# Transposing and weighing attention probabilities later in the slot, in a fused encoder-decoder layer

## The reference, cut to what matters

```
x = x + attention(q, k, v of layernorm(x), mask_self) @ w_ao + b_ao
x = x + attention(q of layernorm(x), k and v of ctx, mask_cross) @ w_co + b_co
x = x + gelu(layernorm(x) @ w1 + b1) @ w2 + b2

attention: scores = q.k / sqrt(32); scores = scores * mask - 10000 * (1 - mask)
           softmax(scores over keys) . v, head by head
```

## Time and profile before

| what | value |
|---|---|
| median of three runs | 1813.92 us (1811.06 to 1816.85) |
| profiled execution, its own time | 1812.26 us |
| its span, first to last instruction | 1810.4 us |
| TensorE (PE) busy | 1702.9 us, 94% |
| VectorE (DVE) busy | 1030.0 us, 57% |
| ScalarE (ACT) busy | 1039.1 us, 57% |
| GpSimd (POOL) busy | 658.4 us, 36% |
| mean granted TensorE clock | 0.987 of 2.4 GHz |

### The profile page before, as it was taken

The page is one execution under the profiler, slowest core; times in us unless marked ns, Lnnn a source line. Parts: engine busy times, 40 slices in busy tenths (PEclk is TensorE's granted clock), DMA queues, the critical chain, the costliest instruction groups (busy, mean ns, idle before and its releaser), DMA issues. The chain is left out here.

```text
span 1810.4 us, 40174 instructions
## 1 busy us (share of the span) xinstructions
PE 1702.9 (94%) x13342; PEld 1035.0 (57%) x13342; DVE 1030.0 (57%) x3584; ACT 1039.1 (57%) x3138; POOL 658.4 (36%) x812
## 2 busy tenths in 40 slices
PE   3899999999988999999999986999999999999999
PEld 2567676767656766766766653444444444444444
DVE  6877777777765677777777763633232333324221
ACT  3577787778876777777778864532323232323332
POOL 0456565565644554554655642202020202010110
PEclk9999999999999999999999996999999999999999
DMA  4432222222221232332223221320101010102010
GB/s 137 120 111 75 87 96 87 86 83 86 92 76 51 75 109 87 109 108 89 97 91 98 86 68 52 124 70 12 58 12 58 12 58 12 64 6 70 0 47 24
DMA packets 83236, 130.31 MB, mean 72 GB/s; under 512 B 14144, under 2 KB 22336, under 8 KB 83136
## 3 DMA queue, kind: packets, MB, share of 16 engines
q1 hardware_dynamic: 83136, 129.04, 22.3%
HBM read 103.83 MB, written 25.17 MB: 71 GB/s over the span
## 5 line engine op out<-in xcount | busy, mean ns | idle before, releaser
L1239 POOL TENSOR_TENSOR a_p_s<-a_p_s,a_rcp 128x512 f32<-128x512 f32 x256 | 266.0, 1039 | 479.3 <-DVE a_rcp L886 479.2
L755 ACT ACTIVATE a_p_s<-a_t_s,a_mx 128x128 f32<-128x128 f32 x1024 | 398.6, 396 | 9.7 <-DVE a_mx L877 9.7
L1420 PE MATMUL m_ps_y<-w,m_g_r 128*128 128x512 f16 x1536 | 353.2, 379 | 0.0
L1406 PE MATMUL m_ps_h<-mlp_xT,w 128*128 128x512 f16 x1536 | 349.8, 379 | 1.7 <-PEq L407 1.7
L1505 DVE SCALAR_TENSOR_TENSOR m_g_r<-m_g_t,up_by,m_g_r 128x512 f16<-128x512 f32 x128 | 103.2, 806 | 406.6 <-ACT m_g_r L1478 406.3
L1406 PEld LDWEIGHTS m_ps_h<-mlp_xT,w 128*128 128x128 f16 x1536 | 150.2, 98 | 181.6 <-issue 2.2
L1420 PEld LDWEIGHTS m_ps_y<-w,m_g_r 128*128 128x128 f16 x1536 | 150.3, 98 | 176.5
L877 DVE CUSTOM_DVE_ANT_0 a_t_s<-a_ps_s,a_m_add 128x128 f32<-128x128 f32 x1024 | 230.6, 281 | 6.4 <-DVE a_ps_s L867 6.1
L1461 ACT ACTIVATE m_g_t<-m_ps_h,bias_cols,back 128x512 f32<-128x512 f32 x128 | 99.3, 776 | 222.6 <-PE m_ps_h L1406 222.6
L867 DVE TENSOR_TENSOR a_ps_s<-a_ps_s,a_m_mul 128x512 f32<-128x512 f32 x256 | 176.4, 689 | 58.8 <-PE a_ps_s L539 58.5
L746 ACT COPY a_pT<-a_ps_t 128x512 f32<-128x512 f32 x256 | 148.8, 581 | 103.1 <-PE a_ps_t L548 103.0
(11 more groups left out here) (118 smaller groups left out, 2267.7 us busy)
## 6 DMA issues: line engine op xcount, KB each, us to landing
w_stage<-in_w SPq DMA_DIRECT2D x64, 256.0 KB, 3.1
a_x_t<-in_x SPq DMA_DIRECT2D x32, 256.0 KB, 2.8
a_res_t<-in_x SPq DMA_DIRECT2D x32, 256.0 KB, 2.9
x_after_self<-a_y_t SPq DMA_DIRECT2D x32, 256.0 KB, 2.0
w_stage<-in_ctx SPq DMA_DIRECT2D x32, 256.0 KB, 2.9
a_x_t<-x_after_self SPq DMA_DIRECT2D x32, 256.0 KB, 2.8
a_enc_t<-in_ctx SPq DMA_DIRECT2D x32, 256.0 KB, 3.4
a_res_t<-x_after_self SPq DMA_DIRECT2D x32, 256.0 KB, 2.8
```

Of the source, the lines that this page charges most:

```text
L755: last = nc.scalar.activation(p_s[:, n % 2, j], t_s[:, n % 2, j], ACT.Exp, scale=-1.0, bias=mx[:, n % 2, j:j + 1], accum_out=sums[:, n % 2 ...
L1239: nc.gpsimd.tensor_tensor(p_s[:, n % 2], p_s[:, n % 2], rcp[:, n % 2].unsqueeze(2).to_broadcast([P, HQ, P]), ALU.mult).then_inc(s["normal" ...
L1406: last = nc.tensor.matmul(ps_h[j % 2][:], w1[hw][:, j // KC, kc, (j % KC) * P:(j % KC + 1) * P], xT[:, hx, kc], start=(k == 0), stop=(k == ...
L1420: last = nc.tensor.matmul(ps_y[b][:], g_r[:, j % 2, hg, b * P:(b + 1) * P], w2[hw][:, j // KC, j % KC], start=(j == 0 and x == 0), stop=(j ...
```

## The change

Seven things are moved:

- `p_s`, `sums` and `rcp` get four places (`KC`) in place of two, and `exponent`, `invert_sums` and `normalise` wait for the slot four before in place of two before.
- `transpose_probs` handles slot n - 3 and comes in the middle of the slot, after the first half and the first flips.
- `weigh_values` comes at the end of slots 6 and 2, after the second half or the queries.
- ScalarE: `exponent` first, then the copy of keys, then `copy_probs`; `high_context` after the copies of values and queries.
- VectorE: `invert_sums` of slot 1 before `output_row`; `low_context` after the flip and the look; the statistics of the first row of a group move from slot 0 to slot 7 of the group before; the norms of group 1 move from before slot 0 of group 0 into it.
- `flips`: in the last group of self-attention the flips of x move ahead of the second half; at the end of attention the two last pairs move ahead too.
- SyncE: the two loads of x, both in slot 7 before, come in slots 5 and 7.

```diff
-            p_s = buf("p_s", [P, 2, HQ, P])
+            p_s = buf("p_s", [P, KC, HQ, P])
...
-                    return [("x", *at_end[g, n])] if last and (g, n) in at_end else []
+                    return [("x", *inside[g, n])] if not last and (g, n) in inside else []
...
-                    return [("x", g + 1, n - 2), ("enc", g + 1, n - 2)] if last and n in (2, 3) else []
+                    return [("enc" if last else "x", g + 1, n - 2)] if n in (2, 3) else []
...
-                        if n == 7 and norms_ahead(g + 1):
+                        if n in (5, 7) and g != -1 and norms_ahead(g + 1):
...
-                            load_x(g + 3, 0)
-                            load_x(g + 3, 1)
+                            load_x(g + 3, b)
...
-                        if n == 2 and prev or n == 6 and cur:
-                            for k in range(KC):
-                                weigh_values(*lag(g, n, 6 - k))
                         for what, k, b in flips(g, n, nxt, False):
                             (flip_x if what == "x" else flip_enc)(k, b)
+                        if cur if n >= 3 else prev:
+                            transpose_probs(*lag(g, n, 3))
...
-                        if cur if n >= 2 else prev:
-                            transpose_probs(*lag(g, n, 2))
+                        if n == 2 and prev or n == 6 and cur:
+                            for k in range(KC):
+                                weigh_values(*lag(g, n, 6 - k))
...
-                        if n >= 2 or known(g, 1):
-                            act.wait_ge(s["pt_done"], at(slot_no(*lag(g, n, 2))))
-                            act.wait_ge(s["inverted"], at(slot_no(*lag(g, n, 2))))
+                        if n >= KC or known(g, 1):
+                            act.wait_ge(s["pt_done"], at(slot_no(*lag(g, n, KC))))
+                            act.wait_ge(s["inverted"], at(slot_no(*lag(g, n, KC))))
...
-                        if cur if n >= 3 else prev:
-                            copy_probs(*lag(g, n, 3))
                         if cur if n >= 1 else prev:
                             exponent(*lag(g, n, 1))
                         if n >= 4 and nxt:
                             copy_cols(g + 1, n - 4, WK, k_t, "k_done", "k_copied")
-                        if n == 2 and prev:
-                            high_context(g - 1, 1)
-                        if n == 6 and cur:
-                            high_context(g, 0)
+                        if cur if n >= 3 else prev:
+                            copy_probs(*lag(g, n, 3))
...
+                        if n == 2 and prev:
+                            high_context(g - 1, 1)
+                        if n == 6 and cur:
+                            high_context(g, 0)
...
-                        if ahead and g != -1:
+                        if (g, n) == (0, 0):
+                            statistics(1, 0)
+                            for k in (0, 1, 4, 5, 6, 7):
+                                norm_part(1, k)
+                        elif (g, n) == (0, 2):
+                            statistics(2, 0)
+                            norm_part(2, 0)
+                        elif (g, n) == (0, 3):
+                            norm_part(2, 1)
+                        elif ahead and g != -1 and (g, n) != (0, 1):
                             norm_part(g + 2, n)
-                        elif ahead and n == 7:
-                            for k in range(NS):
-                                norm_part(1, k)
+                        if n == 7 and g != -1 and norms_ahead(g + 1):
+                            statistics(g + 3, 0)
```

More of the change, by code:

```diff
@@ L293, in flips @@
                 if not nxt:
-                    at_end = {(gN - 1, 4): (gN, 0), (gN - 1, 5): (gN, 1), (gN, 0): (gN + 1, 0), (gN, 1): (gN + 1, 1)}
-                    return [("x", *at_end[g, n])] if last and (g, n) in at_end else []
+                    inside = {(gN - 1, 4): (gN, 0), (gN - 1, 5): (gN, 1), (gN, 0): (gN + 1, 0), (gN, 1): (gN + 1, 1)}
+                    return [("x", *inside[g, n])] if not last and (g, n) in inside else []
                 if not crosses(g + 1):
@@ L498, in slot @@
                             load_res(g, n // 6)
-                        if n == 7 and norms_ahead(g + 1):
+                        if n in (5, 7) and g != -1 and norms_ahead(g + 1):
+                            b = n // 7
                             if isinstance(g, int) and g in (NG - 3, gN - 3):
-                                for b in range(GB):
-                                    sp.wait_ge(stored[b], 16 * (NG - 4 if g == NG - 3 else NG + 3))
-                            load_x(g + 3, 0)
-                            load_x(g + 3, 1)
+                                sp.wait_ge(stored[0], 16 * (NG - 4 if g == NG - 3 else NG + 3))
+                                sp.wait_ge(stored[1], 16 * (NG - 4 if g == NG - 3 else NG + 3))
+                            load_x(g + 3, b)
                         if (g, n) == (0, 0):
@@ L510, in slot @@
                         pass_piece(g, n)
+                        if (g, n) == (0, 0):
+                            load_x(2, 0)
+                            load_x(2, 1)
                     for b in range(GB):
@@ L547, in transpose_probs @@
                         for j in range(HQ):
-                            last = nc.tensor.transpose(ps_t[:, j], p_s[:, n % 2, j], ident[:])
+                            last = nc.tensor.transpose(ps_t[:, j], p_s[:, n % KC, j], ident[:])
                         last.then_inc(s["pt_done"], 1)
@@ L955, in slot @@
                             scale_scores(g, n)
+                        if n == 1 and prev:
+                            if cur:
+                                dve.wait_ge(s["scaled"], at(slot_no(g, n)))
+                            invert_sums(*lag(g, n, 2))
                         if n in (1, 4) and prev:
@@ L961, in slot @@
                             dve.sem_inc(s["mask_begun"], 1)
-                        if n % KC and (cur if n >= 2 else prev):
+                        if n % KC and (cur if n >= 2 else prev and n != 1):
                             if cur:
@@ L967, in slot @@
                             mask_scores(g, n)
+                        for what, k, b in flips(g, n, nxt, False):
+                            (flip_x if what == "x" else flip_enc)(k, b)
+                        if cur or prev or n < 4:
+                            split_weights(g, n)
                         if n == 2 and prev:
@@ L971, in slot @@
                             low_context(g, 0)
-                        for what, k, b in flips(g, n, nxt, False):
-                            (flip_x if what == "x" else flip_enc)(k, b)
-                        if cur or prev or n < 4:
-                            split_weights(g, n)
                         for what, k, b in flips(g, n, nxt, True):
@@ L979, in slot @@
                             split_weights(g, n)
-                        if ahead and g != -1:
+                        if (g, n) == (0, 0):
+                            statistics(1, 0)
[7 more added lines that the diff above has]
+                        elif ahead and g != -1 and (g, n) != (0, 1):
                             norm_part(g + 2, n)
-                        elif ahead and n == 7:
-                            for k in range(NS):
-                                norm_part(1, k)
+                        if n == 7 and g != -1 and norms_ahead(g + 1):
+                            statistics(g + 3, 0)
                     def norm_part(g, n):
                         if n == 0:
-                            statistics(g, 0)
                             statistics(g, 1)
@@ L1256, in slot @@
                             prepare_mask(g + 1, 0)
-                        if n == (2 if g != -1 else 7) and norms_ahead(g):
+                        if (g, n) == (0, 0):
+                            root(1, 0)
+                            root(1, 1)
+                        if n == (2 if g != 0 else 4) and g != -1 and norms_ahead(g):
                             root(g + 2, 0)
```

18 lines of the change are left out of this document (9 added, 9 removed).

## The result

The changed kernel takes 1853.62 us (median of 4 runs, 1852.74 to 1859.39), the kernel before 1813.78 beside it (4 runs, 1811.06 to 1816.85): a ratio of 1.0226, 95% interval 1.0199 to 1.0252. It is slower, as forecast, but by 40 us and not by 14; 1853.6 lies above the range of 1813 to 1841. All of it is in the attention part: from the first product of the feed-forward part to the end both kernels take 684 us.

A forecast was written before the change was run, and what follows sets the result against it. TensorE's queue was taken to set the pace. Regular groups 23.5, plus 1.8 + 3.4 + 0.4 - 0.8 - 1.1 - 2.9 - 2.5 - 7.5, sum to +14.3 us: forecast 1828, range 1813 to 1841.

The forecast's parts named there:

- (a): Slot 3: outputs of b = 1 wait 1.60 us after weighing for the context; net +1.20 self, +1.11 cross a group.
- the clock falls in each group: Rival: recurring waits slow TensorE's clock, 1.5 us lost in each of 29 groups, 44 more, 1872 us; chance 0.05.
- (b): Scores wait 1.00 us for the last queries' copy, with no transposition left to cover it: +0.44 us in every group.
- (c): First queries wait for `y_done`, and a transposition now stands between: -0.30 us in self, -0.15 in cross groups.
- (d): TensorE's wait for GpSimd ends with half a slot more and four places: -0.95 us cross, -0.20 self a group.
- (e): Cross groups: second encoder flip comes long after the first, so its wait goes: -0.43 us, and -0.20 for smaller edges.
- (f): Slot 1 of cross: values wait for slot 0's flip, whose copy follows `copy_probs`: a new gap of 0.85 us.
- (g): Seven groups with a weight split on ScalarE: +0.25 us each, 1.8; also groups 14, 30 and 31: +3.4.
- (h): Opening: first scores' masking now comes ahead of group 1's norms: -1.1 us, bounds 0 and -3.7.
- (i): Change of stage: waits in groups 15 and 16 go, bias products run at full clock: -2.9 and -2.5 us.
- (j): End of attention: last scores to last outputs take 23.8 us instead of 31.3: -7.5, bounds -4 and -11.
- the ends give back more: Rival: full clock lasts through opening, change of stage and end; another 12 us come back, 1816 us; chance 0.12.

## Why the prediction fell short, step by step

**The step that failed is (a)**, twice over. Its bounds were "1.5 (both engines at once on it) to 1.8 (each finishing another copy, 0.1 each)". The wait is 2.13. I asked what ScalarE would be busy with when the weighing ends, and not what it would be waiting for: the instruction in front of the context was itself released by the weighing, so a whole copy (0.5) stands behind the event and not a rest of one. With the copy behind the context the wait was 1.67 and both periods came out as forecast to 0.05 (32.50 for 32.45, 34.02 for 34.03). In groups 1 to 13 and 17 to 29 this is 6.0 + 6.4 = 12 us.

Its second half is a rival that the prediction held at 0.05: **the clock falls in each group**. It did, in 9 of groups 1 to 13 and in none of 17 to 29, at 1.6 a time: 14.5 to 15 us. The price of 1.5 was right; 29 groups and 1872 were too many. A clock below 1.00 in the steady part was also one of the prediction's own signs of being wrong. It set the rival aside because "single gaps of 1.49 left the clock at full in places", and that was half of what its rows say. The gap of 1.49 before 539.97 left it at full (1.00 from 541 to 544), but behind the same gap before 546.74 the clock fell, in the kernel before:

```profile
547.00:549.00 2.00, 2.00 (x32) 1.74 (x34) 0.72 (x2) 1.45 (x4) 0.00 (x0) 0.54 0.04 8
```

Thirty-two products of scores took 2.09 there in place of 1.17.

The Trainium skill, "TensorE: Matmul & The Clock Gate", section "HAM oscillation — how this bites in real kernels", describes a loop in which a wait for DMA of about 3 to 5 us slows the clock anew in every round. The waits here are shorter than those, so the 1872 that the prediction puts down to that rule does not follow from the page. The trace shows the same kind of loss at 1.99 to 2.06 idle in 9 self groups (0.78 and 0.65 in the windows behind one wait); in groups 17 to 29, and in groups 1 to 13 with 1.60 or less idle, it shows none (1.00).

**(b)** The 1.00 in front of the scores came as forecast. That it would be the queries' copy alone was half the truth: VectorE's maxima became just as late, through the context of slot 6, to which no step had given a price. **(c)** Right: the queries of slot 4 follow the transposition at once in self, with 0.2 in cross. **(d)** Right: GpSimd's share of TensorE's waits is 3.9 in place of 31.2. What it missed is that a part of this gain was to be had by inverting the sums first, without moving anything on TensorE: alone, that took these waits from 31.2 to 23.7 and the kernel to 1799. **(e)** No second wait of an encoder flip is left in the steady part, as forecast. **(f)** 0.91 for 0.85; undone by itself, 0.92 a period.

**(g)** The 3.4 for groups 14, 30 and 31 is a slip: with their neighbours' prices it would be 1.14 + 0.67 + 0.67 = 2.5. Groups 30 and 31 took 3.1 more than before; with the context first, groups 1 to 13 took 13.8 more than before and 17 to 29 took 8.9 more, against 14.8 (with a little more for the split groups) and 8.7. **(h)** Nothing came back: +0.5 to the first scores of group 1, where -1.1 and +0.4 were forecast. TensorE did get to the bias products sooner (51.74, at full clock), but stood 3.90 later, at the x flip of 59.69. **(i)** The bias products do run at full clock, but the stretch from group 14 to 17 gave 1.8, with 4.3 forecast; each of the three groups has the longer context wait in it. **(j)** 22.5 where 23.8 was worked out, and the last products at full clock give 2.0 more: -10.8 for -7.5. The nearness of 22.5 and 23.8 is partly luck: 23.8 was worked out at half clock, and in this stretch the clock was down for a part only (1.00 from 1140 to 1145, 0.71 from 1145 to 1150, 0.98 from 1150 to 1165). The rival **"the ends give back more"** was thus right about the full clock in the bias products and the last products, but the opening gave nothing back for it.

The distance of 27 us is thus: values' copy +12.4, clock +14.7, change of stage +2.5, opening +1.2, end -3.3: +27.5, for 41.0 - 14.3 = 26.7 to explain. The 0.8 between them is left to the small terms.

The rival **"the wait of (a) is covered"** was worth more than its 0.10 as a thing to build: with the wait covered the change is at 1810.7 (the rival had 1798), and at 1797 with the gap of (f) closed too. **"ScalarE becomes the bound"** did not happen: with the same work on ScalarE, the order alone took the kernel to 1824 and in the end to 1779.

## What to carry to other kernels

Where a step is moved to the end of a slot, look at each engine's queue at the instruction in front of the one that reads the result, and ask which event frees that one: if it is the same event, its whole length lies in the wait, and swapping the two can take it out (here 30 us for two lines). The same holds for what stands behind: an engine that waits in order holds back work which feeds a third engine, and it shows as a late release somewhere else (here the maxima, 5 us on). When two releases come at about the same time, undoing one shows little (0.18 of 0.44 a group here); mend both before the cause is called refuted. And take a change apart: this one was 40 us slower as a whole, and held an order of two instructions worth 14 and flips at the ends worth 9.

## What the runs showed of the hardware

Of TensorE's clock: behind an idle time of 1.99 to 2.06 in each of the self groups 1 to 13 of the change it fell in 9 and stayed at full in 4. With 1.60 or 1.47 (a flip before it) and a period of 32.5 it fell in none of them. But the kernel with the weighing alone moved has the same idle time in each self group, with more besides, and its clock fell in 2 of the 13 only, in none of those with a period of 34.13. And in the kernel before, one gap of 1.49 brought it down (546.74) and another one, 7 us earlier, did not (539.97). So the length of one wait does not decide by itself. What does was not settled here; shown is that in this kernel, at this place, shortening the idle time, and with it the period, gave the clock back, twice.
